# Rounding chain of a quantised feed-forward part, rewritten, with its third weight prepared one part earlier

## What is computed

```python
def act_qdq(x):                       # qmax = 2**15 - 1
    scale = jnp.maximum(jnp.max(jnp.abs(x)) / qmax, 1e-12)
    return jnp.clip(jnp.round(x / scale), -qmax - 1.0, qmax) * scale
def fixed_qdq_u16(x):
    scale = 1.0 / 65536.0
    return jnp.clip(jnp.round(x / scale), 0.0, 65535.0) * scale
...
x = act_qdq(x)                                        # x: layernorm of 512 x 256
up = act_qdq(x @ lpbq_dequant(w_up).T)                # 512 x 768
gate = act_qdq(x @ lpbq_dequant(w_gate).T)
sig = fixed_qdq_u16(jax.nn.sigmoid(gate))
gate = act_qdq(gate * sig)
o = act_qdq(gate * up)
return o @ lpbq_dequant(w_down).T                     # w_*: rounded to 4 bits by blocks of 32
```

## Time and profile before

| | us |
|---|---|
| three runs: median (lowest to highest) | 1456.81 (1455.27 to 1457.78) |
| the profiled execution, its own time | 1455.65 |
| its span, first to last instruction | 1453.9 |
| so around the span | 1.75 |

### The profile page before, as it was taken

The page is one execution under the profiler, slowest core; times in us unless marked ns, Lnnn a source line. Parts: engine busy times, 40 slices in busy tenths (PEclk is TensorE's granted clock), DMA queues, the critical chain, the costliest instruction groups (busy, mean ns, idle before and its releaser), DMA issues. The chain is left out here.

```text
span 1453.9 us, 22869 instructions
## 1 busy us (share of the span) xinstructions
PE 1299.6 (89%) x8447; PEld 1003.3 (69%) x8447; DVE 983.6 (68%) x1256; ACT 877.8 (60%) x1562; POOL 245.4 (17%) x245
## 2 busy tenths in 40 slices
PE   4999999999999999899999999999999969887643
PEld 3877787868687878697768687877777733666322
DVE  4657676777767687656777767685858555735476
ACT  5758585857676676565767676675757412534152
POOL 4202021211212120111211212020303022020000
PEclk9999999999999999999999999999999979998776
DMA  4000000000000001200000000000000054261000
GB/s 163 1 1 19 1 19 9 12 19 1 19 1 15 1 19 55 80 1 13 7 19 1 20 1 19 1 20 1 15 1 5 1 169 64 27 80 16 22 0 15
DMA packets 29684, 34.70 MB, mean 24 GB/s; under 512 B 3984, under 2 KB 26000, under 8 KB 29328
## 3 DMA queue, kind: packets, MB, share of 16 engines
q1 hardware_dynamic: 27536, 29.83, 8.0%
q0 software_dynamic: 2048, 3.43, 1.7%
HBM read 25.89 MB, written 0.52 MB: 18 GB/s over the span
## 5 line engine op out<-in xcount | busy, mean ns | idle before, releaser
L463 DVE TENSOR_TENSOR prob_sum<-prob_sum,probs 128x1024 f32<-128x1024 f32 x224 | 264.5, 1222 | 164.6 <-ACT probs L382 163.9
L382 ACT ACTIVATE probs<-scores_a 128x1024 f32<-128x1024 f32 x128 | 131.2, 1025 | 209.1 <-PE scores_a L578 208.1
L315 POOL TENSOR_TENSOR k_split<-prob_sum,k_split 64x512 fp32r<-64x512 f32 x128 | 165.0, 1289 | 303.2 <-ACT prob_sum L358 303.2
L442 DVE TENSOR_REDUCE step_max<-scores_a 128x2 f32<-128x1024 f32 x128 | 156.9, 1225 | 37.3 <-PE scores_a L566 35.5
L442 DVE TENSOR_REDUCE step_max<-scores_b 128x2 f32<-128x1024 f32 x128 | 155.7, 1216 | 0.0
L577 PE MATMUL scores_a<-q_twice,k_split 128*128 128x256 f32 x512 | 139.1, 305 | 5.0 <-ACT q_low_max L373 4.9
L308 POOL TENSOR_TENSOR w_lo<-w_raw,w_hi 128x768 fp32r<-128x768 f32 x16 | 34.9, 2181 | 593.8 <-ACT w_hi L327 593.7
L382 ACT ACTIVATE probs<-scores_b 128x1024 f32<-128x1024 f32 x128 | 131.3, 1026 | 0.0
L577 PE MATMUL scores_b<-q_twice,k_split 128*128 128x256 f32 x512 | 128.4, 283 | 0.0
L578 PE MATMUL scores_b<-q_low_max,k_ones 128*128 128x256 f32 x512 | 127.9, 282 | 0.0
L578 PE MATMUL scores_a<-q_low_max,k_ones 128*128 128x256 f32 x512 | 127.9, 283 | 0.0
(11 more groups left out here) (214 smaller groups left out, 2641.3 us busy)
## 6 DMA issues: line engine op xcount, KB each, us to landing
ctx_rows<-in_ctx_dram SPq DMA_DIRECT2D x10, 512.0 KB, 3.6
w_raw<-in_L_xattn_w_v_dram SPq DMA_DIRECT2D x14, 256.0 KB, 3.2
probs<-in_ctx_dram SPq DMA_DIRECT2D x6, 512.0 KB, 6.1
grouped<-dots_sb SPq DMA_DIRECT2D x16, 136.0 KB
grouped<-dots_sb POOLq DMA_DIRECT2D x16, 136.0 KB, 13.2
w_raw<-in_L_xattn_w_q_dram SPq DMA_DIRECT2D x16, 128.0 KB, 2.3
w_raw<-in_L_xattn_w_k_dram SPq DMA_DIRECT2D x16, 128.0 KB, 2.4
wo_pair<-in_L_xattn_w_o_dram SPq DMA_DIRECT2D x16, 128.0 KB, 2.1
```

What stands on the lines that cost most here:

```text
L315: pool.tensor_tensor(k_split[0:DH, B, keys], k_staged_b[j % 2], k_split[DH:P, B, keys].bitcast(F32), ALU.subtract).then_inc(k_low[B], 1)
L382: act.activation(probs[:, j % 2, h, :], flat_scores[h], ACT.Exp, scale=SCALE).then_inc(exp_done, 1)
L442: dve.tensor_reduce(step_max[:, :, 1 - h, j - 1], scores[h][:, :, :], X, ALU.max).then_inc(max_done, 1)
L463: dve.tensor_tensor(prob_sum[:, h, :], prob_sum[:, h, :], probs[:, j % 2, h, :], ALU.add).then_inc(sum_done, 1)
```

## The change

Five things are done.

1. SP loads the third weight in self attention, ahead of `Wo`. DVE quantises it between the batches, after the last dots copy and ahead of the residual's sum; PE transposes it ahead of the second batch's steps, ACT copies it. All that leaves the feed-forward part.
2. The input is transposed as soon as it is normalised, and rounded as it comes out of PSUM, half by DVE and half by ACT.
3. The maxima are one DVE instruction each, a reduction of absolute values of what ACT copied; ACT's magnitudes go.
4. Rounding is `move` (times the inverse, plus ROUND), `hold` (both bounds, shifted by ROUND) and `back` (minus ROUND, times the scale). The first product and the second take `back` into themselves, as SCALAR_TENSOR_TENSOR: (a - ROUND) x b. The scales that are then left out are put into the next scale, and the last into the sum with the residual. Two thirds of each `move` are ACT's, and all of `up`'s; POOL has only the all-reduces. A one-element sigmoid is put first on ACT.
5. DVE's queue is written in another order: maxima of `up` stand between the rounding of the gate's thirds.

```diff
+                if b == 0:
+                    for part in range(W_PARTS):
+                        if part == 0:
+                            dve.wait_ge(hidden_chain, DOWN * W_OPS)
+                        quantise_weight(dve, part, hidden_w[DOWN], w_scales, hidden_chain, DOWN * W_OPS)
                 for n in range(b * QT, (b + 1) * QT):
                     dve.wait_ge(y_made, n + 1)
...
                 if b > 0:
                     pe.wait_ge(y_added, b * QT)
+                    pe.wait_ge(hidden_chain, 3 * W_OPS)
+                    for k in range(4 * WT_BANKS):
+                        out = down_bank(k // 4)[:, k % 4 * P:(k % 4 + 1) * P]
+                        last = transpose_weight(pe, hidden_w[DOWN], DC, k, out, ident)
...
-            pool.memset(round_bias[:, :], ROUND).then_inc(bias_ready, 1)
             invert_std(pool, moments, power, norm_chain, inverse_std)
+            pool.memset(moves[:, 0:1], ROUND).then_inc(moves_set, 1)
+            pool.memset(moves[:, 1:2], -ROUND).then_inc(moves_set, 1)
             for n in range(5):
...
-                if n == UPS:
-                    pool.wait_ge(hidden_copied, 2 * FC)
-                    pool.wait_ge(scaled, 2 * UPS + 2)
-                    round_pass(pool, UPS, 0, up[:, :, :].rearrange("p c n -> p (c n)")).then_inc(up_chain, 1)
...
+            def move(which, t, src):
+                return dve.tensor_scalar(t, src, inverse_of(which), ROUND, ALU.mult, ALU.add)
+
+            def hold(t):
+                return dve.tensor_scalar(t, t, ROUND + A_MAX, ROUND - A_MAX - 1.0, ALU.min, ALU.max)
+
+            def back(which, t):
+                return dve.tensor_scalar(t, t, ROUND, scale_of(which), ALU.subtract, ALU.mult)
+
+            def largest(which, c, src):
+                dve.tensor_reduce(limits[:, which, c:c + 1], src, X, ALU.max, apply_absolute_value=True
+                                  ).then_inc(peak_read, 1)
...
+                dve.scalar_tensor_tensor(sig[:, c, :], sig[:, c, :], ROUND, gate[:, c, :], ALU.subtract, ALU.mult
+                                         ).then_inc(gated, 1)
...
+            for k, piece in enumerate(thirds):
+                dve.wait_ge(up_moved, k + 1)
+                hold(up[:, piece, :]).then_inc(up_held, 1)
+            find_scale(GATED, unit=U_STEPS)
...
+            for piece in thirds:
+                move(UPS, up[:, piece, :], up[:, piece, :]).then_inc(up_moved, 1)
+            for k, piece in enumerate(thirds):
+                act.wait_ge(up_held, k + 1)
+                act.activation(up[:, piece, :], up[:, piece, :], ACT.Identity, bias=moves[:, 1:2]).then_inc(up_back, 1)
+            act.wait_ge(scaled, SCALED[GATED])
+            for piece in thirds[1:]:
+                move(GATED, sig[:, piece, :], sig[:, piece, :]).then_inc(gated_moved, 1)
```

362 lines of the change are left out of this document (180 added, 182 removed).

## The result

| | us |
|---|---|
| kernel before, median (lowest to highest) | 1456.93 (1455.27 to 1457.78) |
| kernel after, median (lowest to highest) | 1440.24 (1438.07 to 1441.34) |
| ratio, 95% interval | 0.9885 (0.9868 to 0.9902) |
| profiled execution of after; its span | 1439.66; 1437.9 |

What follows compares the result with a forecast made beforehand. Bounds: POOL's waits to change work and a serial DVE chain in the feed-forward part. Terms 2.65 + 13.45 - 1.15 + 0.8 - 0.4 = 15.35 us took 1455.65 to 1440.3, plus 1.16 gave 1441.5; range 1437.5 to 1447.

Steps and rivals of the forecast that it cites:

- Input, +2.65: From 1357.1 to PE's first gate chunk: transposes and reduction hide beside POOL's 5.85 us wait; gain 2.65 us.
- PE's start to the first product, +13.45: From PE's first gate chunk to the first product: 42.8 us before, 29.3 by DVE's new queue; gain 13.45 us.
- 9.5 of it is POOL (6.68 + 2.82): Ahead of the first product: POOL's wait and its rounding of `up` claimed as 9.5 of the 13.45 us gain.
- First product to first tile, -1.15 and -0.4: First product to PE's first last-projection tile: 23.8 us becomes 24.95, loss 1.15; 0.4 more for all-reduces beside DVE.
- the term of 0.4: Two all-reduces beside DVE's two-scalar passes: one side pays, a loss of 0.4 to 0.8 us, taken as 0.4.
- Self-attention, +0.8: Second batch: steps start later but the ninth no longer waits for DMA; gain 0.8, between +1.2 and -2 us.
- Its clock stays up: Self attention, second batch: PE no longer stops for 7 us, so its clock stays up; part of the 0.8 gain.
- Clock 0: Whole kernel: no gain or loss taken for the clock; 1 us allowed on each side of the range.
- Slow instruction forms: Rival: DVE's 31 large absolute-value reductions and products run at half rate, 16.5 us lost, 1458.0 us; chance 0.04.
- A second batch after 1321: Rival: slow PE clock or stretched DVE work starts the ninth step at 1321 or later, 1443.9 us; chance 0.10.
- All-reduces behind all of DVE's queue: Rival: all-reduces wait for DVE's holds and sigmoid passes, costing about 1.5 us instead of 0.4, 1442.6 us; chance 0.06.
- The change doing what it says: Rival denied: another unnamed POOL instruction between the all-reduces would bring back 5.85 us each; no chance given.

Runs made afterwards that it cites:

- experiment 5: Kernel after, with the feed-forward normalisation's inverse deviation made by DVE add, ACT square root and DVE reciprocal instead of POOL's power: 1437.7 us.
- experiment 7: Kernel after, with two more DVE reductions of 128x1536, results unused, right behind the third weight's quantisation in self attention: 1442.85 us.
- Experiment 1: Kernel before, with `up`'s first rounding pass as three DVE passes right after its scale instead of one on POOL: 1451.7 us.
- Experiment 6: Kernel after, with ACT's two moves of the gated product put ahead of the last two of three passes bringing `up` back: 1437.49 us.
- experiment 3: Kernel after, with the third weight loaded, quantised, transposed and copied in the feed-forward part again: 1439.08 us.
- experiment 12: Kernel after, with the edits of experiment 5 and experiment 8 and the third weight quantised and transposed in the feed-forward part again: 1436.36 us.
- experiment 2: Kernel after, with the move of `up` as one POOL instruction again: 1445.85 us.
- experiment 8: Kernel after, with DVE's three holds of `up` behind the gated product's scale instead of ahead of it, and ACT's order to fit: 1439.79 us.
- 5 and 8 joined: Kernel after, with the edits of experiment 5 and experiment 8 together: 1437.12 us.
- experiment 4: Kernel after, with four of six parts of the third weight's quantisation between the halves of DVE's dots copies, two behind: 1441.69 us.

## Why the prediction was right, point by point

**Input, +2.65: measured +2.61.** PE started 12.39 us after the part's start; 12.35 was said. The cover was POOL's, as said: experiment 5 takes the cover away and everything behind moves up by 3.3. The 0.8 us that the lower bound of the range gave to POOL being ready sooner without the weight's load beside it have no ground: they compared two different changes of POOL's work, and the same one took 5.85 us with the load and 5.84 without.

**PE's start to the first product, +13.45: measured +13.70.** The walk through DVE's new queue gave 29.3 us; it took 29.06. The rounding of the gate started 0.5 us nearer to PE's first chunk, as said. PE's clock was at 0.50 for the first 5.9 us, as before; where it came up sooner the same instructions took less, down to 27.95 us (experiment 7). The size was right, but the sentence behind it, "9.5 of it is POOL (6.68 + 2.82)", was wrong. The 9.5 us are the length of POOL's stretch and not what it cost in the old order: 3.6 us of DVE's sigmoid passes lay under it, and 2.0 more would have been DVE's had POOL not done the pass. Experiment 1 shows 4.2. The sum did not suffer, because it was made from DVE's queue and not from POOL's rows; anyone who had asked for the POOL edit alone on the strength of that sentence would have been promised more than twice what it brings.

**First product to first tile, -1.15 and -0.4: measured -1.21.** All-reduces beside DVE's passes do get longer (0.72 and 1.15), by more than the term of 0.4 assumed: 1.2 us together. Still nothing comes on top. The third ended at 1397.24, before DVE's last pass over the sigmoid did (1397.78). The three holds of `up`, from 1405.44 to 1407.24, end after the stretched all-reduce, and they were already in the forecast loss of 1.15. What is hidden under work that is itself on the path isn't added to it, so the 0.4 had no place in the sum. DVE's 1.38 and 0.44 us of waiting for ACT were in the sum as well. Experiment 6 shows that it is not ACT's order that makes them.

**Self-attention, +0.8: measured +1.18; one half of the term held, the other was luck.** The nine instructions stand from 1294.22 to 1304.1, the ninth step comes at 1320.02 (1318.5 to 1321 was said) and waits for no transfer, and experiment 7 shows the cover gone. The half that held is that the steps are not stopped and filled again, for which the prediction had at most 1.2 us. From the ninth step to the feed-forward part it took 37.70 us before and 36.60 after. That repeats: 36.6 in all eight profiles in which the weight stands where the change puts it, and 37.6 to 38.7 in the four with the old placement (before, experiments 1, 3 and 12).

The other half is when the ninth step starts, and there the size was set against one late transfer. With the old placement that step waited 6.91, 4.13, 4.65 and 7.25 us for its transfer and started 45.2, 42.4, 42.9 and 45.6 us behind the last copy of the first batch. With the new one it started 45.1 to 46.5 us behind it, leaving out the kernel with two more passes and the one whose clock fell. In the pair of profiles the two starts happen to agree (45.22 and 45.14). Over the groups the later start eats the gain: the whole stretch took 82.9, 80.05, 81.6 and 83.2 us with the old placement and 81.7 to 83.1 in six kernels with the new one (after, experiments 2, 5, 6 and 8, and 5 and 8 joined). The means are 81.9 and 82.2. I took the +0.8 from one pair; by the groups it is about nothing.

```profile
1305.06 2.79 PE L743 MATMUL bank<-ident,wide 128*128 128x128 f32 x12 [4.43 <-DVE x_res L1176]
1307.65 2.66 PE L1251 MATMUL bank<-grouped,kron 128*128 128x32 f32 x12
...
1320.02 0.78 PE L1251 MATMUL bank<-grouped,kron 128*128 128x160 f32 x4
```

These rows of the kernel after show the new chain: PE waits for DVE's sum behind the quantisation, transposes, and starts the second batch at 1307.65, 7.1 us after 1300.59. "Its clock stays up" was right only from the ninth step on. PE had idled for 6.91 us ahead of that step before, and had been at work after. These are the 4.6 us from its start on, before first, then after:

```profile
1319.40:1324.00 4.60, 4.59 (x21) 4.57 (x22) 2.43 (x11) 1.26 (x6) 0.00 (x0) 0.57 0.00 0
```
```profile
1320.02:1324.62 4.60, 4.09 (x30) 3.80 (x31) 3.91 (x17) 3.37 (x15) 0.00 (x0) 1.00 0.00 2
```

Ahead of that step the clock was down in the kernel after too. In the window from 1306 to 1317 it was at 0.50:

```profile
1306.00:1317.00 11.00, 10.46 (x49) 10.30 (x48) 6.00 (x29) 6.18 (x26) 0.00 (x0) 0.50 0.45 62
```

PE had done little for the 4.4 us before. At this clock it was busy for 10.46 of the 11 us, and the eight steps took 12.4 us where 11.9 was said. How much of the 0.5 us is the clock's was not measured apart; in experiment 7, where it was back at 0.91 in the window from 1315.2 to 1318.2, 6 us behind the first of them in place of 9, they took 11.8.

The third weight's load cost nothing, as said. It landed 11.0 us after its issue at 1176.5, so at about 1187.5 (1187.0 was said), and DVE's first copy of a projection came 19.28 us after its first instruction of the self-attention, as against 19.44 before.

**Clock 0: measured +0.42** in the last projection, where the granted clock 3 to 6 us behind the first tile was 0.80 before and 0.97 after. The -0.70 lies ahead of the changed code: the self-attention starts 0.76 us later (1169.72 and 1168.96). Neither belongs to the change. No run shows the 1 us that the range gives the clock on each side. What the runs showed is 14.64 to 16.33 us from the first tile to the end, and 27.8 to 29.2 us from PE's first chunk to the first product, with the granted clock at 1.00 to 0.50 and at 0.92 to 0.50 in the windows 3 to 6 us behind their starts.

**The rivals.** Slow instruction forms: the reduction of absolute values over 512 columns took 0.68 and SCALAR_TENSOR_TENSOR 0.68, the price of the plain forms in the kernel before (0.69 and 0.68); dead. The 0.53 us for each in that rival is an estimate, what 512 columns more cost a plain reduction by the earlier trace rows: half of 1.741 less 0.69. A second batch after 1321: not in this run, although PE did stay at the slow clock through most of the first eight steps, which was that rival's condition. It was there when the kernel after ran again: the ninth step started at 1324.26, behind the stretch at 0.57 of the clock. All-reduces behind all of DVE's queue: no; the longest was 1.15. The change doing what it says: one wait of 5.84 us on POOL and no other.

## What to carry to other kernels

Price an engine's stretch by the wait of who needs it and by what lies under it, never by its own length: 9.5 us of POOL were worth 4.2 us in the old order, and its pass would have cost 6.4 us in the new one. Build the sum from the queue of the engine that paces, instruction by instruction; it held to 0.4 us in each of the three feed-forward stretches, while the term that rested on one observed wait for a DMA was met by luck in part. And where single profiles of one kernel differ by 4 us, compare stretches between events, not spans: the feed-forward part repeated within 0.1 us (81.28 and 81.35) while the spans were 1437.9 and 1442.2. Then look at the clock of each stretch: in experiment 4 the same part took 82.4 us, 1.5 us of it more in the last projection.

## What the runs showed of the hardware

- From the end of POOL's own last instruction to an all-reduce whose maximum was ready by then it took 5.77 to 6.08 us in 14 of 15 cases and 7.02 in one (experiment 12). From an all-reduce to POOL's own pass over `up` it took 7.12 us (before) and 7.28 (experiment 2); the 6.68 of the earlier trace rows count from the scale, which came later. The price came at each such change. Toward the all-reduce it ran from the end of the last instruction, whether the operand had been ready for 3.1 us (after, 5.84) or for 0.6 (experiment 5, 5.86); in the other direction no run separates this.
- An all-reduce of 0.35 us takes 0.72 beside passes over the sigmoid and 1.15 beside the holds of `up`; three DVE passes took 1.89 us beside it as elsewhere. In the earlier trace rows four DVE passes took 2.32 us in place of 1.38 beside memsets of POOL, and did so in the kernel after too. What decides which of the two grows is not shown.
- The granted clock fell in stretches of the same code in some executions: 0.83 to 0.87 or 0.91 or 1.00 between 20 and 40 us, 0.57, 0.93 or 1.00 between 1276 and 1292. One such fall cost 5 us, a third of what the whole change brought. What sets it off in one execution and not in another stays open; no run here separates it.
- How soon the granted clock came up went with the length of two stretches. Over all 14 profiles it was 0.50 to 1.00 in the window 3 to 6 us behind the first tile of the last projection, and from that tile to the end of the span it took 16.33 us at the lowest and 14.64 us at the highest. Over the kernels with the rewritten part it was 0.50 to 0.92 in the same window behind PE's first chunk, and the first product came 29.2 to 27.8 us after that chunk.
- The transfers that fill `grouped` ended at different times from run to run, with waits from 4.1 to 7.25 us at the same step in the four kernels with the old placement.
